# Decoder block with routed experts: logits out of the output projection, expert 0 gathered by TensorE, five experts fetched ahead

## The reference, cut to what matters

```python
out = softmax(scores) @ V                      # cross attention
return out @ Wo.T + bo                         # x = layernorm(x + this)

logits = xt @ wg                               # xt: 2048 x 128, wg: 128 x 8
gates_k, idx_k = top_k(softmax(logits), 2)     # gates divided by their sum
locs = cumsum(one_hot(choices)) - 1            # place of a pair in its expert, all first choices first
valid = loc < 512                              # capacity of an expert
disp[idx, loc] += xt * valid                   # 8 experts x 512 rows
out = relu(disp @ w1 + b1) @ w2 + b2
y = sum_k gates_k * valid * out[idx_k, loc]
```

## Time and profile before

| | us |
|---|---|
| median of 3 runs | 444.09 (440.9 to 446.13) |
| the profiled execution, its own time | 440.14 |
| its span in the trace | 438.3 |
| outside the span | 1.84 |
| busy in the span: PE, PEld, DVE, ACT, POOL | 365.4, 260.5, 257.0, 194.5, 188.2 |
| mean granted PE clock, share of full speed | 0.926 |

### The profile page before, as it was taken

One profiled execution on the slowest core, in us unless ns is written; L12 is line 12 of the kernel. 1 busy time (PEld: TensorE's weight loads), 2 busy tenths in 40 slices (PEclk: granted clock), 3 DMA queues, 4 the chain that ended last, 5 costly groups with the idle time before them and its releaser, 6 DMA issues.

```text
span 438.3 us, 8261 instructions
## 1 busy us (share of the span) xinstructions
PE 365.4 (83%) x3249; PEld 260.5 (59%) x3249; DVE 257.0 (59%) x742; ACT 194.5 (44%) x333; POOL 188.2 (43%) x232
## 2 busy tenths in 40 slices
PE   6999988999989999881489978797857988888780
PEld 2677775677767777761238756752635656765550
DVE  0788992689999899759600100022785788437430
ACT  1567775734577777521244433022362432124420
POOL 2234546853343520310376777772333437440002
PEclk9999999999999999995599999899889887859996
DMA  7999600000000000030011111117000000010000
GB/s 275 408 406 396 209 4 1 2 1 1 1 1 2 1 2 1 10 89 0 18 55 42 55 50 52 50 54 198 9 0 1 0 2 0 25 72 1 1 1 12
DMA packets 18358, 27.54 MB, mean 63 GB/s; under 512 B 2416, under 2 KB 13680, under 8 KB 17680
## 3 DMA queue, kind: packets, MB, share of 16 engines
q1 hardware_dynamic: 16208, 22.69, 14.5%
q0 software_dynamic: 2112, 4.33, 3.4%
HBM read 20.59 MB, written 6.42 MB: 62 GB/s over the span
## 4 chain that ended last, share of the span: by engine, by line
PE 57%; POOL 11%; DVE 11%; ACT 9%; issue 6%; DMA 4%; POOLq 0%; SPq 0%; DVEq 0%; ACTq 0%
PE bank L410 7%; PE bank L433 7%; PE bank L420 7%; PE bank L576 6%; POOL choice_rows L730 4%; POOL q_diag L716 4%; PE bank L589 3%; PE bank L995 3%; PE bank L863 3%; PE bank L988 2%; PE bank L814 2%; PE bank L393 2%; ACT x_tok L1310 2%; DMA q_diag<-in_q_self 1%; PE bank L872 1%
## 5 line engine op out<-in xcount | busy, mean ns | idle before, releaser
L576 PE MATMUL bank<-mask_bf,ident_bf 128*128 128x512 bf16 x206 | 59.5, 425 | 4.5 <-DVE mask_bf L1442 3.4
L493 DVE TENSOR_REDUCE neg_max<-bank 128x16 f32<-128x1024 f32 x34 | 41.5, 1222 | 19.4 <-PE bank L410 19.3
L383 POOL TENSOR_TENSOR scratch<-k_comp,con 128x512 f32<-128x512 f32 x32 | 33.4, 1047 | 37.6 <-PE bank L410 33.8
L465 ACT COPY probsT<-bank 128x1024 f32<-128x1024 f32 x34 | 34.4, 1012 | 26.3 <-PE bank L420 26.2
L716 POOL DMA_INDIRECT q_diag<-token_rows,place x32 | 30.8, 963 | 35.4 <-DVE place L1634 26.0
L476 ACT ACTIVATE probs<-probs 128x1024 f32<-128x1024 f32 x34 | 35.9, 1056 | 19.6 <-DVE probs L520 19.6
L433 PEld LDWEIGHTS bank<-v_pair,probsT 128*64 128x64 f32 x1088 | 34.7, 138 | 16.4 <-issue 10.8
L433 PE MATMUL bank<-v_pair,probsT 128*64 128x18 f32 x1088 | 37.9, 212 | 5.5 <-ACT probsT L465 4.6
L1665 DVE TENSOR_TENSOR probsT<-bank,mb 128x512 f32<-128x512 f32 x7 | 4.8, 691 | 62.2 <-PE bank L995 62.2
L410 PE MATMUL bank<-scratch,q_diag 64*128 64x256 f32 x272 | 39.5, 410 | 0.7 <-DVE scratch L383 0.5
L566 POOL TENSOR_SCALAR var_e<-mv 128x4 f32<-128x4 f32 x28 | 6.9, 247 | 75.8 <-DVE mv L1686 41.0
(11 more groups left out here) (281 smaller groups left out, 678.8 us busy)
## 6 DMA issues: line engine op xcount, KB each, us to landing
mw<-in_mw SPq DMA_DIRECT2D x2, 2048.0 KB, 14.0
v_pair<-in_v_self SPq DMA_DIRECT2D x4, 576.0 KB, 11.2
q_diag<-in_q_self SPq DMA_DIRECT2D x4, 512.0 KB, 10.4
choice_rows<-hT SPq DMA_DIRECT2D x1, 2048.0 KB, 13.3
con<-in_const SPq DMA_DIRECT2D x1, 1249.5 KB, 15.1
k_comp<-in_k_self SPq DMA_DIRECT2D x4, 256.0 KB, 9.3
x_tok<-in_x SPq DMA_DIRECT2D x1, 1024.0 KB, 10.8
ctxT<-in_ctxT SPq DMA_DIRECT2D x1, 1024.0 KB, 9.6
```

What stands on the lines that cost most here:

```text
L383: mult(k_heads[:, i % 2], k_comp[:, i, :, None, :].to_broadcast([P, 2, HG, S]), hm, ALU.mult).then_inc(s["spread"], 1)
L465: nc.scalar.copy(probsT[:, i % 2], bank[:, 4:6, :].rearrange("p a n -> p (a n)")).then_inc(s["evacuated"], 1)
L493: have_m = link.mark(nc.vector.tensor_reduce(m, sc, AX, ALU.max, negate=True))
L576: nc.tensor.matmul(bank[:, bk, :], ident_bf[:, :], mask_bf[:, 0, None, :].to_broadcast([P, 8, S]), start=True, stop=True)
```

## The change

1. **Fold.** PE makes `ones * wg`, and turns `wo` and `bo` (behind self attention). DVE forms the centred router weights in `with_x = [ident | wg - mean]`, and PE multiplies `wo` and `bo` by them, so that `with_o = [wo | wo wg']` and `logit_bias`. These exchanges stand in quad 0 of the FFN loop: PE waits twice (`folded` 1 and 2) between `keys_values(0)` and L863, and DVE does its part behind L1472 and behind `values_out(0)`.
2. **Projection.** For each tile PE issues a product of `xT` (the residual) with `with_x`, then one of the attention output with `with_o` on top, 136 columns each. DVE adds `bo` and, with a second small instruction, the logits' bias. `x_side` and `add_bo` go. The logits are then those of the tokens before norm 4, without the division by their deviation: the gates' gap is multiplied by `rstd` afterwards.
3. The turns, copies and products for the logits go (L589, L595, L915 of norm 4). ACT now normalizes all four quads. Quad 3's residual goes through ACT (copy out of the bank) and POOL (add of `bo`), and its statistics come behind the choice of experts.
4. **Ranks.** The counts are one accumulation of two bfloat16 products. The capacity test moves: a row over it falls in no slot's tile. `rank_hot`: chunks 0 and 1 on DVE, chunk 2 on ACT (8 squares, one ReLU), chunk 3 by a subtraction on POOL and a comparison on DVE.
5. **Expert 0** is not gathered: for each of 16 token tiles DVE writes a one-hot 128 x 512 (`first_hot`, three buffers) and PE adds `x_tok[:, t]` times it into bank 6, which takes the place of `turn_in(0)` and of `keep(5, 10)`. `place[:, 0]` is released first; the gates, their exponential and `slots` 2 come behind the 16 one-hots.
6. `AHEAD = 5`: experts 1 to 5 are gathered ahead. `token_rows` has a zero row in front.

```diff
@@ SP, POOL
+            sp.dma_start(token_rows[0:1, :], hT[0:1, 0, 0, 0:D]).then_inc(s_moe["zeroed"], 16)
...
-            att_spread(pool, att["cross"], NT, cross_keys, add_bo, first=2)
-            ln_pool(pool, ln["ln4"], link)
+            att_spread(pool, att["cross"], NT, cross_keys, last_rstd, first=2)
+            for q in range(NQ):
+                if q == NQ - 1:
+                    pool.wait_ge(s_oTs, NQ + 1)
+                    tt(work[:, NT - 4:NT], work[:, NT - 4:NT], rows[:, 6:7].to_broadcast([P, 4, D]), ALU.add).then_inc(s_side, 1)
+                rstd_of(pool, ln["ln4"], q, link)
+            pool.wait_ge(s_r["rows"], 1)
+            tt(rank_hot[:, 24:32], row_index_bf[:, None, :].to_broadcast([P, 8, P]),
+               route("row_of", TOPK * NT)[:, 24:32, None].to_broadcast([P, 8, P]), ALU.subtract).then_inc(s_r["rows"], 1)
...
             pool.wait_ge(s_r["slots"], 1)
-            for e in range(AHEAD):
+            for e in range(1, AHEAD + 1):
                 fetch(e)
+            pool.wait_ge(s_r["slots"], 2)
@@ PE
+            mm(bank[:, 4, 0:E], con_at("ones"), wg[:, :], start=True, stop=True)
+            tr(bank[:, 4, P:2 * P], wo[:, :], ident)
+            tr(bank[:, 4, 2 * P:3 * P], rows[:, 6], ident).then_inc(s_r["fold"], 1)
...
                 keys_values(q)
+                if q == 0:
+                    pe.wait_ge(s_r["folded"], 1)
+                    mm(bank[:, 4, 3 * P:3 * P + E], wo_turned, with_x[:, P:], start=True, stop=True)
+                    mm(bank[:, 4, 3 * P + E:3 * P + 2 * E], bo_turned, with_x[:, P:], start=True, stop=True).then_inc(s_r["fold"], 1)
...
+                else:
+                    pe.wait_ge(s_r["folded"], 2)
...
-                    last = mm(cols4(2 + q, j), masked(q)[:, j * P:(j + 1) * P], wo[:, :], start=True, stop=True)
+                    if j % 2:
+                        residual(q, j)
+                    last = mm(projection(q)[:, j // 2, j % 2], masked(q)[:, j * P:(j + 1) * P], with_o, start=False, stop=True)
...
+            def residual(q, j):
+                t = 4 * q + j
+                mm(projection(q)[:, j // 2, j % 2], xT[:, t * P:(t + 1) * P], with_x, start=True, stop=False)
...
-            keep(2, 12)
+            keep(6, 16)
             pe.wait_ge(s_r["chosen"], 1)
...
+            keep(2, 16)
...
+            for t in range(NT):
+                if t % 4 == 0:
+                    pe.wait_ge(ln["ln4"]["y"], ln["ln4"]["tiles"] + t + 4)
+                pe.wait_ge(s_r["hot"], TOPK * NT // 8 + t + 1)
+                last = mm(bank[:, 6, :], x_tok[:, t], first_hot(t), start=t == 0, stop=t == NT - 1)
...
-            keep(5, 10)
-            turn_in(0)
             hidden(0)
@@ DVE
+            dve.wait_ge(s_r["fold"], 1)
+            stt(with_x[:, P:], bank[:, 4, 0:E], -1.0 / P, wg[:, :], ALU.mult, ALU.add)
+            cp(wo_turned, bank[:, 4, P:2 * P])
+            cp(bo_turned, bank[:, 4, 2 * P:3 * P]).then_inc(s_r["folded"], 1)
+            cp(with_x[:, 0:P], ident)
+            cp(with_o[:, 0:P], wo[:, :])
...
                 values_out(q)
+                if q == 0:
+                    dve.wait_ge(s_r["fold"], 2)
+                    cp(with_o[:, P:], bank[:, 4, 3 * P:3 * P + E])
+                    cp(logit_bias, bank[:, 4, 3 * P + E:3 * P + 2 * E]).then_inc(s_r["folded"], 1)
...
+            for t in range(NT):
+                if t >= 3:
+                    dve.wait_ge(s_r["found"], t - 1)
+                ts(first_hot(t), first_slots, wanted[:, t:t + 1], None, ALU.is_equal).then_inc(s_r["hot"], 1)
+            link(tt(route("e", NT), route("m1", NT), route("m0", NT), ALU.subtract))
+            tt(route("e", NT), route("e", NT), rstd[:, :], ALU.mult).then_inc(s_r["gap"], 1)
+            dve.wait_ge(s_r["exp"], 2)
...
```

More of the change, by code:

```diff
@@ L347, in build @@
         s_oT, s_oTs, s_wo = sem("s_oT"), sem("s_oTs"), sem("s_wo")
-        s_r = names("route", "logits", "chosen", "ranks", "gap", "exp", "slots", "rows", "hot", "found")
+        s_r = names("route", "logits", "chosen", "ranks", "gap", "exp", "slots", "rows", "hot", "found", "fold", "folded")
         s_moe = names("experts", "zeroed", "stored", "turned", "xT", "out")
@@ L592, in ln_act @@
         def ln_act(act, s, quad, other=None):
[L593 removed]
+            act.wait_ge(s["yT"], s["turns"] + quad + 1)
             banks = s.get("banks", (6, 7))
@@ L911, in cross_queries @@
                     pe.wait_ge(s_v_free, NQ)
-            def logits(q):
-                pe.wait_ge(ln["ln4"]["yT_out"], ln["ln4"]["quads"] + q + 1)
-                for t in range(4 * q, 4 * q + 4):
-                    last = mm(bank[:, 0, t * E:(t + 1) * E], xT[:, t * P:(t + 1) * P], wg[:, :], start=True, stop=True)
-                return last
             def turn_out(q):
@@ L1317, in _ @@
             norm_act("ln4", 1)
-            for q in range(NQ):
-                ln_act(act, ln["ln4"], q)
+            act.wait_ge(s_r["logits"], NQ)
+            cp(tiles22(work[:, NT - 4:NT]), projection(NQ - 1)[:, :, :, 0:P]).then_inc(s_oTs, 1)
+            norm_act("ln4", 2)
+            act.wait_ge(s_r["rows"], 1)
+            for n in range(16, 24):
+                off = link.mark(A(rank_hot[:, n], row_index_bf[:, :], ACT.Square, bias=route("row_of", TOPK * NT)[:, n:n + 1], scale=-1.0))
+            link.wait(off)
+            A(rank_hot[:, 16:24], rank_hot[:, 16:24], ACT.Relu, bias=con_at("ones")[:, 0:1], scale=-1.0).then_inc(s_r["exp"], 1)
+            norm_act("ln4", 3)
             act.wait_ge(s_r["gap"], 1)
@@ L1534, in projected @@
                 dve.wait_ge(s_wo, q + 1)
-                dve.wait_ge(s_side, NQ + q + 1)
-                n = link.mark(tt(work[:, r], bank[:, 2 + q].rearrange("p (t n) -> p t n", n=P), x_side[:, r], ALU.add))
+                n = link.mark(tt(tiles22(work[:, r]), projection(q)[:, :, :, 0:P], tiles22(bo4), ALU.add))
+                logits(q).then_inc(s_r["logits"], 1)
                 told_quad(ln["ln4"], q, [n] * 4)
@@ new lines, in _ @@
+            a, late, own = route("tot", E * CT), route("run", E * CT), route("at", E * CT)
+            wanted, n_of = route("gate", NT), route("c", NT)
+            link(tt(wanted, v_at[:, 0:NT, 0], v_at[:, NT:, 0], ALU.add))
+            link(tt(n_of, chosen_bf[:, 0:NT, 0], chosen_bf[:, NT:, 0], ALU.add))
+            link(stt(wanted, n_of, float(-TOPK * T), wanted, ALU.mult, ALU.add))
+            for j in range(CT):
+                link(ts(first_slots[:, j * P:(j + 1) * P], con_at("row_index"), float(j * P - TOPK * T), None, ALU.add))
```

216 lines of the change are left out of this document (113 added, 103 removed).

## The result

Changed: 449.16 us median of 4 runs (448.47 to 451.0); before, beside it: 440.9 (438.62 to 444.09). The ratio is 1.019, 95% interval 1.0135 to 1.0244: slower, and whether by more than 2% is not settled. Forecast 451.5, range 444.5 to 458. The profiled execution took 448.47 us, its span 446.6, where the forecast in own time was 449.5.

What follows compares the result with a forecast made beforehand. No engine alone was the bound, but a chain of waits judged place by place. 10.25 + 1.35 - 0.8 - 1.4 = +9.4 gave 449.5 on the profiled execution, 453.5 on the median; forecast 451.5 us between, range 444.5 to 458.

Steps and rivals of the forecast that it cites:

- Wait for the fold: FFN loop, quad 0: PE waits for DVE's folded weights, L863 starts at 86.1 in place of 75.85, +10.25 us.
- rival (b): FFN loop: the early wait is absorbed by waits of later quads, not slower, 440 in forecast terms; chance 0.07.
- Clock behind it: PE's work after the fold wait: 2.7 us at half clock rate lose 1.35 us, bounds 0 and 2.7.
- the first part: Fold wait and the clock behind it together, ahead of cross attention: +11.6 us.
- Cross attention: Without L709 a DVE instruction is no longer held and PE's 0.80 us wait goes: -0.8 us.
- projection with logits: Last projection ends later, but the search for the two best starts near 188.4 instead of 193.47: -5.1 us.
- Top-2 to the first gather: Routing from the top-2 search to the first gather: -1.1 us, with POOL's new instructions holding DVE 1.0 and 2.0.
- Rival (a): Routing keeps its lead: POOL's two instructions hold nobody, PE stays warm, -5.8 us from 176 us on; chance 0.20.
- Rival (d): Routing: holds eat all of the 6.3 us, list not shorter, 458 us in forecast terms; chance 0.07.
- Expert 0: One-hot products, then ACT's exposed line with table loads: `hidden(0)` at 227.65, 5.6 us later than before.
- Rival (c): ACT's line ahead of `hidden(0)` is dearer, by a drain or a table for the squares: +2.8 us; chance 0.12.
- Experts: Experts stage: POOL's last scatters end at 295.7 instead of 297.08, -1.4 us for all from 176 us on.

Runs made afterwards that it cites:

- chip 12: Another chip, where the changed kernel was run again unaltered: 449.94 us, ratio 1.026 to the kernel before.
- c: Kernel before plus only the fold and its two waits, results unused: 468.23 us, ratio 1.036 to the kernel before.
- b: Changed kernel with 35 and 9 unused PE products in front of the two fold waits: 465.63 us, ratio 1.031 to the kernel before.
- f: Changed kernel with POOL's chunk of the rank one-hots back on DVE: 466.67 us, ratio 1.018 to the kernel before.
- d: Changed kernel with the gates' gap and ACT's line moved ahead of the 16 one-hots: 468.38 us, ratio 1.036 to the kernel before.
- m: Changed kernel with gates' gap and ACT's line ahead of the 16 one-hots, repeated on another chip: 470.5 us, ratio 1.035 to the kernel before.
- g: Changed kernel with unused PE products between the list's parts and ahead of the one-hot products: 447.32 us, ratio 1.019 to the kernel before.
- h: Changed kernel with fold early, ACT's line early, POOL's chunk on DVE and PE kept busy: 430.89 us, ratio 0.988 to the kernel before.
- l: Changed kernel with DVE's fold instructions moved ahead of its wait for quad 3's rstd: 457.02 us, ratio 1.003 to the kernel before.

## Why the prediction was right, step by step

The mechanism and the sign were right: the early wait costs more than the routing gains. That the total came so close was in part luck. By the stages the change costs 10.2 to 11.0 us where the sum said 9.4, and the profiled execution came out 1 us below its forecast because its start was 2.7 us shorter than that of the kernel before, which the change does not explain; with equal starts it would have been 1.6 us above. The terms:

- **Wait for the fold.** Forecast +10.25 by the DVE row that could not start before 82.85. L863 started as quad 0 became ready (75.78, 75.85), L898 10.1 us behind: +10.2 in the first profile and +10.1 on chip 12. c shows that the shift passes whole, as the chain of the earlier trace rows said; rival (b), absorption, is dead.
- **Clock behind it.** Forecast +1.35, measured 2.3 (6.15 - 3.84; b gives 2.4). This is the term that was mis-sized: I took the recovery of 2.7 us from the one place of the earlier trace rows, as if it were the same everywhere. Here it was 4.9. It is not even the same from run to run: with the same waits L898 took 5.62 us in f and 6.57 in d, so this term is 1.8 to 2.7. With the wait, the first part is +12.4 against +11.6.
- **Cross attention**, -0.87 for -0.8, and **projection with logits**, -5.06 for -5.1: right.
- **Top-2 to the first gather.** Beside POOL's two instructions DVE lost 0.64 and 1.54 us for 1.0 and 2.0. With the chunk's cheap comparison, 0.42 for 0.35, the stage came out at -2.1 in place of -1.1. Rival (a), that they hold nobody, falls by the two rows, and f takes the larger away. Rival (d), no shorter list, falls by the stages: from the last turn to the first gather they are 7.2 us shorter (5.06 + 2.14).
- **Expert 0.** List to `hidden(0)`: forecast 20.85, measured 236.84 - 214.80 = 22.0. Its parts are the ones named, and two were shown by taking them away: ACT's line 3.3 (m; 2.9 between g and h), cold products 2.9 (g, 16.76 - 13.90; forecast 1.35, the same mis-sized term). Rival (c) asked for a drain: L1382's load starts at 233.21, lasts 1.28, and the instruction starts at 234.51. Nor does a load stand ahead of the squares (L1366, at 205.08): the only one before 231.46 is at 0.72. The Trainium skill (ScalarE: Activation LUTs, "What ACT_TABLE_LOAD costs") has a drain of about 1380 ns beside the load; this trace disagrees with it, since 0.02 us pass between load and instruction, as that of before did.
- **Experts.** Forecast -1.4 for all from 176 us on, measured -0.6. The clock took 1.5 more than forecast at the one-hot products and 1.1 more at L1032 (6.12 us, 3.70, forecast 1.35), and the shorter list gave 1.0 back; that makes 1.6, and where the other 0.8 was saved was not traced.

Of the points that would have shown me wrong none came. One detail did not come as written: in front of L898 PE idles 1.59 us and not 7, since most of the wait is in front of the first fold product.

## What to carry to other kernels

Before folding weights "for free" beside other work, look where the engine that has to do it stands in its own stream: five tiny DVE instructions behind a wait for POOL stopped PE for 9 us, and the same instructions a few lines earlier stopped it for 1.4. Look also at what the first products behind a wait will cost: here they ran at half clock for up to 5.6 us, and products whose results nobody uses, issued during the wait, gave that back (2.4 us in b, 2.9 in g). When a step is moved behind a list, move nothing with it (here the gates and the table loads) that used to hide under the transfers.

## What the runs showed that I had not expected

- How long PE keeps its low clock once it works without a gap differed from place to place, and not by how long it had been idle. It was 4.9 us at 83.28 and 5.6 at 215.68, each behind some 10 us with only 1.0 and 2.2 us of short products, but also 4.9 at 236.84, behind 4 us with 0.8 us of them. It was 2.7 in the earlier trace rows behind 2.79 us of idleness, and 2.6 in the kernel before at 216.91, behind 21 us with some 5 us of short products (the row below: clock 0.61, so 2.4 GHz from about 219.6). What sets it is open. With fillers in the wait, b had a granted clock of 1.00 from 78 to 90 us.

```profile
218.00:220.00 2.00, 2.00 (x7) 0.77 (x6) 0.23 (x3) 0.00 (x0) 1.59 (x2) 0.61 0.24 64
```

- POOL's additions do not hold every DVE instruction. Beside L732 (198.08 to 199.37) the reduction L1638, from SBUF to SBUF, took 0.29 us, and only L1639 behind it lasted about to POOL's end. Beside L707 (80.08 to 81.34) the copies L1527 and L1528 out of a bank took 0.28 each, and only L1529, a copy from SBUF, lasted about to POOL's end.
- On two of the three chips of the experiments the experts stage stalls. In l, at 261 to 267 us, PE's products of one expert come about 0.7 us apart with no semaphore as releaser, and DVE and ACT show waits at the same time:

```profile
262.84 0.27 PE L1039 MATMUL bank<-mw,hT 128*128 128x128 f32 x1 [1.05 <-issue]
...
264.98 0.55 PE L1039 MATMUL bank<-mw,hT 128*128 128x128 f32 x2 [1.06 <-issue]
...
270.81 0.58 ACT L1392 COPY probs<-bank 128x512 f32<-128x512 f32 x1 [7.97 <-remote]
270.91 0.69 DVE L1735 TENSOR_TENSOR probsT<-bank,mb 128x512 f32<-128x512 f32 x1 [13.74 <-remote]
```

The clock then falls to 0.50 and a second loss follows. What holds the engines there was not found, and it stays open. Stage D of the kernels with one-hot products is 103 to 109 us on these chips, and 81 to 90 on the other two.
